# One-hot blocks of a token sort written by VectorE in three operations, row one-hots eight at a time, and the output stored in four groups

## The reference, cut to what matters

```python
x = x + 0.5 * expert_choice(layernorm(x))      # stage 0: 8 experts pick tokens
x = x + patch_attention(layernorm(x))          # stage 1
x = x + 0.5 * expert_choice(layernorm(x))      # stage 2
x = x + 0.5 * token_choice(layernorm(x))       # stage 3: each token picks experts
x = x + relative_attention(layernorm(x))       # stage 4
x = x + 0.5 * token_choice(layernorm(x))       # stage 5
```

```python
probs = softmax(flat @ gate_W.T)               # 2048 x 8
top_v, top_i = top_k(probs, 2)                 # two experts per token
out_e = (silu(flat @ w1_e) * (flat @ w3_e)) @ w2_e      # 128 -> 512 -> 128
routed = sum over the two chosen experts of top_v * out_e
shared = the same form with one always-used expert of 512 hidden features, over 8
return 0.5 * shared + 0.5 * routed
```

## Time and profile before

| | |
|---|---|
| Median of 3 runs | 1127.78 us (1127.55 to 1131.54) |
| Profiled execution, its own time | 1131.04 us |
| Its span in the trace | 1129.3 us |
| PE busy | 898.4 us (80%) |
| DVE busy | 715.5 us (63%) |
| ACT busy | 454.3 us (40%) |
| POOL busy | 290.8 us (26%) |
| Mean granted TensorE clock | 0.893 of full speed |

### The profile page before, as it was taken

One profiled execution on the slowest core, in us unless ns is written; L12 is line 12 of the kernel. 1 busy time (PEld: TensorE's weight loads), 2 busy tenths in 40 slices (PEclk: granted clock), 3 DMA queues, 4 the chain that ended last, 5 costly groups with the idle time before them and its releaser, 6 DMA issues.

```text
span 1129.3 us, 22080 instructions
## 1 busy us (share of the span) xinstructions
PE 898.4 (80%) x7931; PEld 701.7 (62%) x7931; DVE 715.5 (63%) x2297; ACT 454.3 (40%) x800; POOL 290.8 (26%) x384
## 2 busy tenths in 40 slices
PE   3599946676664999588999966678888868899995
PEld 3388833444452888567888853345444456788885
DVE  6677666877746777863444446788888556344443
ACT  1133314667621335331455521355455532255542
POOL 7200001000010001338766411000000014866631
PEclk9999965999965999778999995799999867999998
DMA  7700000000000000100111120000000010011113
GB/s 228 241 2 1 1 0 1 2 2 1 2 1 0 1 2 1 38 1 6 49 42 46 28 77 1 1 1 2 1 2 1 2 38 1 10 47 44 46 25 112
DMA packets 27687, 31.27 MB, mean 28 GB/s; under 512 B 5951, under 2 KB 20166, under 8 KB 27584
## 3 DMA queue, kind: packets, MB, share of 16 engines
q1 hardware_dynamic: 22592, 20.55, 6.0%
q0 software_dynamic: 4992, 9.32, 3.0%
HBM read 22.51 MB, written 8.26 MB: 27 GB/s over the span
## 4 chain that ended last, share of the span: by engine, by line
PE 55%; DVE 27%; ACT 8%; POOL 6%; issue 3%; DMA 0%; DVEq 0%
PE bank L1095 8%; PE banks0to L541 6%; POOL stacks_and_choice L947 6%; DVE score_max L1305 4%; PE banks0to L1057 4%; PE banks0to L549 4%; PE banks0to L1058 4%; PE banks0to L1059 4%; PE bank L1081 4%; PE bank L560 3%; PE bank L1548 3%; ACT stacks_and_choice L1464 2%; PE banks0to L1528 2%; PE banks0to L1533 2%; ACT hidden L1459 2%
## 5 line engine op out<-in xcount | busy, mean ns | idle before, releaser
L785 DVE TENSOR_TENSOR hidden<-silu_gate,banks0to 128x512 f32<-128x512 f32 x110 | 75.5, 686 | 156.4 <-PE banks0to L1059 155.0
L1477 ACT ACTIVATE normed_T<-banks0to 128x1024 f32<-128x1024 f32 x80 | 82.4, 1030 | 104.6 <-PE banks0to L1533 104.6
L1095 PE MATMUL bank<-l_w,hidden 128*128 (+1 forms) x880 | 118.3, 278 | 2.7 <-ACT hidden L994 2.7
L1095 PEld LDWEIGHTS bank<-l_w,hidden 128*128 128x128 f32 x880 | 111.2, 195 | 13.5 <-ACT hidden L994 3.7
L994 ACT COPY hidden<-bank 128x512 f32<-128x512 f32 x110 | 64.6, 587 | 134.1 <-PE bank L1081 134.1
L1305 DVE TENSOR_REDUCE score_max<-banks0to 128x8 f32<-128x1024 f32 x80 | 97.6, 1220 | 20.5 <-PE banks0to L1533 18.4
L187 POOL TENSOR_TENSOR ln_rstd<-ln_var_eps,minus_half 128x4 f32<-128x4 f32 x24 | 24.6, 1027 | 305.0 <-DVE ln_var_eps L180 305.0
L969 POOL DMA_INDIRECT l_ffn_results<-normed_T,v_tokens x78 | 78.4, 1005 | 73.6 <-DVE normed_T L806 42.8
L988 ACT ACTIVATE silu_gate<-banks0to 128x512 f32<-128x512 f32 x110 | 65.9, 599 | 63.8 <-PE banks0to L1059 61.9
L957 POOL DMA_INDIRECT stacks_and_choice<-l_ffn_normed,v_tokens x78 | 75.8, 972 | 28.7 <-issue 22.8
L418 DVE SCALAR_TENSOR_TENSOR expert_sum<-bank,gate,expert_sum 128x128 f32<-128x128 f32 x224 | 62.7, 342 | 28.0 <-PE bank L560 28.0
(11 more groups left out here) (252 smaller groups left out, 1967.9 us busy)
## 6 DMA issues: line engine op xcount, KB each, us to landing
l_w<-in_L_ffn_w_e SPq DMA_DIRECT2D x2, 2048.0 KB, 13.7
stacks_and_choice<-l_ffn_results SPq DMA_DIRECT2D x8, 512.0 KB, 6.4
l_w<-in_L_ffn_w SPq DMA_DIRECT2D x1, 2048.0 KB, 11.2
l_ffn_normed<-stacks_and_choice SPq DMA_DIRECT2D x8, 256.0 KB, 2.3
stacks_and_choice<-l_ffn_normed,v_tokens POOLq DMA_INDIRECT x78, 2.5
l_ffn_results<-normed_T,v_tokens POOLq DMA_INDIRECT x78, 2.3
x_tokens<-in_L_attn_x SPq DMA_DIRECT2D x4, 256.0 KB, 3.6
out_x<-x_tokens SPq DMA_DIRECT2D x1, 1024.0 KB, 5.1
```

The lines of the kernel that those rows point to most:

```text
L785: v.tensor_tensor(net.hidden[:, i % 2, :], net.sil[:, i % 2, :], net.bank[2 + i % 2], ALU.mult).then_inc(self.gated.sem, 1)
L1095: ins = mm(net.bank[5 + i % 2][:, 0:D], net.hiddenT[:, i % 2, f, :], w2, start=(f == 0), stop=(f == FT - 1))
L1477: nc.scalar.activation(net.pT[:, i % 2, :, :], net.scores[:, 1], ACT.Exp).then_inc(self.exps.sem, 1)
```

## The change

VectorE takes over the block one-hots. At the end of `token_choice` it compares all 32 choices' blocks with the 39 block numbers in one operation (a 128 x 32 x 39 result, written where the transposed activations lay), and multiplies that once with the choices' numbers and once with their weights; the second product raises `placed`. GpSimd's loop is gone, and the moves' operand is no longer a ring: all 32 block one-hots stand at once. The row one-hots are written eight at a time by one `tensor_tensor` of 128 x 8 x 128, with both inputs broadcast; from the second time on it waits for the eight moves before. The moves wait once for `placed` and once per eight for the row one-hots.

To make room, the buffer of fetched blocks now shares its place with both one-hots. The output is stored in four transfers of four tiles each, each behind its own group's sum.

```diff
     v = net.carve(net.late[:, 0:net.choice_at + CHOICE_WORDS - 2 * F],
-                  dict(normed=(P, T * D, FP32), block_rows=(P, FETCHED * D, FP32), block_T=(P, 2 * 2 * P, FP32),
-                       at_row=(P, RING * P, FP32), in_block=(P, RING * 2 * BLOCKS, FP32)))
-    at = T * D + FETCHED * D
+                  dict(normed=(P, T * D, FP32), block_T=(P, 2 * 2 * P, FP32), at_row=(P, RING * P, FP32),
+                       in_block=(P, T * TOP * 2 * BLOCKS, FP32)))
+    at = T * D
...
+    after = T * D + 2 * 2 * P
+    net.block_rows = net.late[:, after:after + FETCHED * D].rearrange("p (s d) -> p s d", s=FETCHED)
...
+    net.which_block = net.xnT[:, 0:T * TOP * BLOCKS].rearrange("p (c b) -> p c b", c=T * TOP)
...
+    def group_done(self, g):
+        return self.added.sem, self.added.at(0, (3, 5, 7, 8)[g])
...
-        def at_row(c):
-            t, k = c // TOP, c % TOP
-            if c >= RING:
-                dve.wait_ge(self.moved.sem, self.moved.at(0, c - RING + 1))
-            v.tensor_scalar(net.at_row[:, c % RING, :], net.row_numbers[:, :], net.choice_row[:, t, k:k + 1], None,
-                            ALU.is_equal).then_inc(self.at_row.sem, 1)
+        def at_rows(r):
+            if r:
+                dve.wait_ge(self.moved.sem, self.moved.at(0, r * RING))
+            row = net.choice_row[:, :, :].rearrange("p t k -> p (t k)")[:, r * RING:(r + 1) * RING]
+            v.tensor_tensor(net.at_row[:, :, :], net.row_numbers[:, :].unsqueeze(1).to_broadcast([P, RING, P]),
+                            row.unsqueeze(2).to_broadcast([P, RING, P]), ALU.is_equal).then_inc(self.at_row.sem, 1)
...
         for i in range(2, 6):
             step(i)
-            for c in range((i - 2) * RING, (i - 1) * RING):
-                at_row(c)
+            at_rows(i - 2)
...
-        v.reduce_sum(net.choice_gate[:, :, 0], by_tile[3], AX.X).then_inc(self.placed.sem, 1)
+        chain(v.reduce_sum(net.choice_gate[:, :, 0], by_tile[3], AX.X))
+        every = [P, T * TOP, BLOCKS]
+        flat = lambda c: c[:, :, :].rearrange("p t k -> p (t k)").unsqueeze(2).to_broadcast(every)
+        chain.then_wait(v.tensor_tensor(net.which_block, net.block_numbers[:, :].unsqueeze(1).to_broadcast(every),
+                                        flat(net.choice_block), ALU.is_equal))
+        v.tensor_tensor(net.in_block[:, :, 0, :], net.which_block, flat(net.choice_number), ALU.mult)
+        v.tensor_tensor(net.in_block[:, :, 1, :], net.which_block, flat(net.choice_gate),
+                        ALU.mult).then_inc(self.placed.sem, 1)
...
-        pool.wait_ge(self.placed.sem, self.placed.at(0, 1))
-        for c in range(T * TOP):
-            t, k = c // TOP, c % TOP
-            if c >= RING:
-                pool.wait_ge(self.moved.sem, self.moved.at(0, c - RING + 1))
-            for value, dst in ((net.choice_number, net.in_block[:, c % RING, 0, :]),
-                               (net.choice_gate, net.in_block[:, c % RING, 1, :])):
-                ins = g.tensor_scalar(dst, net.block_numbers[:, :], net.choice_block[:, t, k:k + 1],
-                                      value[:, t, k:k + 1], ALU.is_equal, ALU.mult)
-            ins.then_inc(self.in_block.sem, 1)
...
-            pe.wait_ge(self.at_row.sem, self.at_row.at(0, c + 1))
-            pe.wait_ge(self.in_block.sem, self.in_block.at(0, c + 1))
+            if c == 0:
+                pe.wait_ge(self.placed.sem, self.placed.at(0, 1))
+            if c % RING == 0:
+                pe.wait_ge(self.at_row.sem, self.at_row.at(0, c // RING + 1))
...
-            sp.wait_ge(*net.ready)
-            sp.dma_start(out.rearrange("b (a p) d -> p (b a) d", p=P), net.x[:, :, :]).then_inc(stored, 16)
-            sp.wait_ge(stored, 16)
+            for g, stored in enumerate(stores):
+                at = slice(g * GROUP, (g + 1) * GROUP)
+                sp.wait_ge(*made[-1].group_done(g))
+                sp.dma_start(out.rearrange("b (a p) d -> p (b a) d", p=P)[:, at, :], net.x[:, at, :]).then_inc(stored, 16)
+            for stored in stores:
+                sp.wait_ge(stored, 16)
```

More of the change, by code:

```diff
@@ L628, in token_buffers @@
     v = net.carve(net.late[:, 0:net.choice_at + CHOICE_WORDS - 2 * F],
-                  dict(normed=(P, T * D, FP32), block_rows=(P, FETCHED * D, FP32), block_T=(P, 2 * 2 * P, FP32),
-                       at_row=(P, RING * P, FP32), in_block=(P, RING * 2 * BLOCKS, FP32)))
-    at = T * D + FETCHED * D
+                  dict(normed=(P, T * D, FP32), block_T=(P, 2 * 2 * P, FP32), at_row=(P, RING * P, FP32),
+                       in_block=(P, T * TOP * 2 * BLOCKS, FP32)))
+    at = T * D
     net.normed_rows = v["normed"].rearrange("p (t d) -> p t d", t=T)
     net.back_rows = net.late[:, 0:T * TOP * D].rearrange("p (t k d) -> p t k d", t=T, k=TOP)
-    net.block_rows = v["block_rows"].rearrange("p (s d) -> p s d", s=FETCHED)
+    after = T * D + 2 * 2 * P
+    net.block_rows = net.late[:, after:after + FETCHED * D].rearrange("p (s d) -> p s d", s=FETCHED)
     net.block_T = net.late_rounded[:, at:at + 4 * P].rearrange("p (i s k) -> p i s k", i=2, s=2)
     net.at_row = v["at_row"].rearrange("p (s k) -> p s k", s=RING)
-    net.in_block = v["in_block"].rearrange("p (s i b) -> p s i b", s=RING, i=2)
+    net.in_block = v["in_block"].rearrange("p (c i b) -> p c i b", c=T * TOP, i=2)
+    net.which_block = net.xnT[:, 0:T * TOP * BLOCKS].rearrange("p (c b) -> p c b", c=T * TOP)
     net.results = net.xnT[:, 0:SLOTS * D].rearrange("p (s d) -> p s d", s=SLOTS)
@@ L722, in __init__ @@
         self.first_block = LEAD
-        self.router_steps = Tally(net, "tokens_router_steps", 38, 1)
+        self.router_steps = Tally(net, "tokens_router_steps", 40, 1)
         self.selected = Tally(net, "tokens_selected", 1, 1)
@@ L726, in __init__ @@
         self.placed = Tally(net, "tokens_placed", 1, 1)
-        self.at_row = Tally(net, "tokens_at_row", T * TOP, 1)
-        self.in_block = Tally(net, "tokens_in_block", T * TOP, 1)
+        self.at_row = Tally(net, "tokens_at_row", T * TOP // RING, 1)
         self.moved = Tally(net, "tokens_moved", T * TOP, 1)
@@ L937, in gpsimd @@
         net, g = self.net, self.net.nc.gpsimd
-        self.in_block.prime(pool)
         self.front.spread.gpsimd(pool)
-        pool.wait_ge(self.placed.sem, self.placed.at(0, 1))
-        for c in range(T * TOP):
-            t, k = c // TOP, c % TOP
-            if c >= RING:
-                pool.wait_ge(self.moved.sem, self.moved.at(0, c - RING + 1))
-            for value, dst in ((net.choice_number, net.in_block[:, c % RING, 0, :]),
-                               (net.choice_gate, net.in_block[:, c % RING, 1, :])):
-                ins = g.tensor_scalar(dst, net.block_numbers[:, :], net.choice_block[:, t, k:k + 1],
-                                      value[:, t, k:k + 1], ALU.is_equal, ALU.mult)
-            ins.then_inc(self.in_block.sem, 1)
         def fetch(b):
@@ L1099, in move @@
         def move(c):
-            pe.wait_ge(self.at_row.sem, self.at_row.at(0, c + 1))
-            pe.wait_ge(self.in_block.sem, self.in_block.at(0, c + 1))
+            if c == 0:
+                pe.wait_ge(self.placed.sem, self.placed.at(0, 1))
+            if c % RING == 0:
+                pe.wait_ge(self.at_row.sem, self.at_row.at(0, c // RING + 1))
             mm(net.bank[7][:, 3 * P:3 * P + 2 * BLOCKS], net.at_row[:, c % RING, :],
-               net.in_block[:, c % RING, :, :].rearrange("p i b -> p (i b)"), start=(c == 0),
+               net.in_block[:, c, :, :].rearrange("p i b -> p (i b)"), start=(c == 0),
                stop=(c == T * TOP - 1)).then_inc(self.moved.sem, 1)
@@ L1813, in build @@
         net.gates_loaded = (net.sem("router_weights_loaded"), 2 * 16)
-        stored = net.sem("stored")
+        stores = [net.sem(f"stored_{g}") for g in range(T // GROUP)]
         net.wqkv0 = net.sb("l0_wqkv", [P, 3 * D])
```

## The result

The changed kernel takes 1110.46 us (median of 4 runs, 1109.25 to 1111.34), beside 1129.66 for the kernel before: a ratio of 0.9819 [0.9801 to 0.9837] (the two medians by themselves divide to 0.983). It is faster by 19.2 us, not by the forecast 29.0, and lies above the range that was given. Run again in a later comparison it took 1110.88.

What follows compares the result with a forecast made beforehand. GpSimd's block one-hots were taken to pace TensorE's moves in both sorts. Gain: 30.3 us from the sorts, minus 4.0 for low clock, plus 2.7 at the store, 29.0: 1098.8 us from 1127.78, range 1094 to 1106.

Steps and rivals of the forecast that it cites:

- the price of a move: TensorE's moves in each sort: eight moves without waiting take 0.99 us at full clock.
- the cost of the low clock: In each sort, 4 us of TensorE work at half clock, costing 2.0 us each, 4.0 in all; bounds 0 and 4.7 each.
- the three turns: TensorE's up, down and transposes between the four groups of moves: 2.73 us per turn at full clock.
- Three block operations of 1.44 us: VectorE's block one-hots of 1248 elements per partition, in front of gated(3): 1.44 us each, 4.2 us together on the path.
- Row one-hots 1.21 us: One VectorE operation per eight moves takes 1.21 us, exposed in the first group, covered by TensorE's turn in the others.
- The cover of the first `turn_rows`: Behind the last move, the first fetch still lands before the first turn_rows, with 2.6 us left; at most 2.5 per stage late.
- Store 2.7 us: At the kernel's end, four 256 KB stores instead of one of 1024 KB gain 2.7 us; bounds 2.8 and 1.5.
- The rival of serial stores: Output stores run one behind the other at 2.3 us each, ending 1.1 us later than before: 1102.6 us; chance 0.06.
- the slow broadcast operations: VectorE's one-hots run at 2.39 ns per element, 11.6 us more in all: 1110.4; chance 0.10, shared with a longer low clock.
- Full clock: Rival: the clock does not fall in the sorts, or only briefly; 33.0 us gained, 1094.8 us; chance 0.20.
- the lasting low clock: Rival: the gap drops the clock and denser work does not restore it; 1306 us if all blocks stay low; chance 0.02.

Runs made afterwards that it cites:

- single-pass run: Changed kernel with both one-hots written and read as float32r, so a move is one matmul instruction instead of two: 1102.05 us.
- the fastest kernel here: Changed kernel with block one-hots written by groups of eight choices behind gated(3), float32r one-hots, and moves behind the next unit's up and down: 1087.49 us.

## Why the prediction was wrong

The mechanism was right, each wait and the path, and two terms of the sum were too small: the price of a move and the cost of the low clock. Both lie between L914 and the last move: 25.97 us measured, 20.62 predicted (0.12 of the difference is the later start of the moves and 0.09 the three turns, 2.76 instead of 2.73).

- **The row that was misread: "ten moves without waiting take 1.24 us, so eight take 0.99".** The count behind a row is of instructions. A float32 move is two of them, so those were five moves. Eight take 1.75 us: 4 x 0.76 = 3.0 us per sort. The trace of before gave it away: 64 moves in the two stages stand there as 128 matmuls, and "the last two moves" at 530.01 were one; "two moves per microsecond" after 497 were one move as well.

```profile
L1103 PE MATMUL bank<-stacks_and_choice x128: 233/275/469, 498.2 to 980.2; 128*128 128x78 f32 x128
```

  No range was put around this term, because it seemed measured. The single-pass run shows the other price, 0.82. The Trainium skill ("FP8 and Floating Point Precision", section "TensorE Precision Notes") gives four passes to true FP32 operands; in this trace it is two instructions and 2.1 times the time of `float32r`, for 78 columns, and it is the measured 2.1 that counts here.
- **The size of the low clock: "I take 4 us of work at half clock per sort, which costs 2.0 us each".** It lasted 10 us, 9.3 of them busy. The first moves took 1.92 us more than at full clock and the turn behind them 4.93 instead of 2.76: 4.1 us per sort, 2.1 more than assumed. I had taken the last part of the low stretch before, the one behind the return of dense work; the whole of it, from 501.5, was some 10 us. The upper bound (4.7, half of the 9.5 us that were read) was nearer than the value taken. The Trainium skill ("TensorE: Matmul & The Clock Gate", section "HAM oscillation — how this bites in real kernels") tells of a loop of matmuls whose waits for transfers let the next piece start at the lower clock, and advises to restructure it so that TensorE stays busy. The trace agrees: behind 4.5 us of standing still the clock was 0.51, and the fastest kernel here, in which TensorE waits for 0.3 us, has 1.00.
- The account: 0.12 + 3.04 + 0.09 + 2.09 = 5.3 us per sort, 10.7 in two, and 0.3 at the store: 11.0 us of the forecast gain did not come. The profiled executions differ by 20.8 us, 15.6 in the sorts and 2.4 at the store; the other 2.8 are spread over stretches that the change does not touch, and runs of before differ by 4 among themselves. By the medians the gain is 19.2, short by 9.8; the time is 11.7 above the forecast, because the kernel before also took 1.9 more beside the changed one (1129.66) than the forecast started from (1127.78).
- Three block operations of 1.44 us, 4.2 on the path: 1.45, 1.46 and 1.45, and `gated(3)` starts 4.44 us behind L914's start (500.10 in the trace), predicted 4.37. Right.

```profile
495.87 1.45 DVE L917 TENSOR_TENSOR normed_T<-block_numbers,v_tokens 128x1248 f32<-128x1248 f32 x1
...
500.89 1.21 DVE L829 TENSOR_TENSOR stacks_and_choice<-row_numbers,v_tokens 128x1024 f32<-128x1024 f32 x1
```

- Row one-hots 1.21 us, hidden from the second group on: right, TensorE's only wait for them is 0.3 us. The first group was priced but not questioned; writing them singly is faster.
- The cover of the first `turn_rows` stays: the distance from the last move is 6.72 us in both kernels. Right.
- Store 2.7 us: 2.4. The slowest of the four landed 2.6 us behind its issue. The rival of serial stores, which would have lost 1.1 there, is out.
- Of the rivals, the slow broadcast operations (1110.4) gave the right time for a wrong reason: the operations ran as forecast. Full clock is out by the clock's row; the lasting low clock by its return after 10 us.

What stays open is what sets the length of the low stretch. The same sort code had 10 us in two executions and 7 in a third, each in both of its sorts. How much of it comes of the standing still and how much of what is laid behind it can't be told from one profiled execution of each kernel.

## What to carry to other kernels

Before a count in a profile row becomes a price, set it against the count that the loop in the code must give; a float32 matmul counts twice. When an engine's work moves to another one that stands in front of TensorE's next release, price the standing still twice: its own length, and the low clock behind it, here up to as much again. Split the moved work so that only its first part stands there, and put TensorE's independent work in front of the wait: that, with the cheaper operand type, was worth some 23 us, more than the change itself.

## What the runs showed of the hardware

Matmuls whose result nobody reads, in a gap that has to be waited out anyway, made the kernel 4.8 us faster (0.9776 against 0.9819 of before). A low stretch of 3.5 us followed a standing still of only 2.1 us, in four of four sorts, and one of 0.8 us behind the filling, in three of four. In the kernel before, the clock was 0.50 although TensorE never waited longer than 1.0 us at a time. And the same gap of 4.5 us was followed by 10, 7 or 3.5 us at the lower clock, the 3.5 only where wide matmuls came first.
